# VectorE's remainder moved to the front of its step and GpSimd's half put behind it, in the second and third cross-attention; the three products of a chunk in another order

## The reference, cut to what matters

```python
x = x + L0_xattn(layernorm(x), ctx);  x = x + L0_ffn(layernorm(x))
x = x + L1_xattn(layernorm(x), ctx);  x = x + L1_ffn(layernorm(x))
x = x + L2_xattn(layernorm(x), ctx);  x = x + L2_ffn(layernorm(x))
x = x + L3_xattn(layernorm(x), ctx);  x = x + L3_ffn(layernorm(x))
# a cross-attention, for each batch element b and head h
scores = einsum('qd,kd->qk', q_h, k_h) * scale
out_h  = softmax(scores) @ v_h          # 56 queries, 1500 keys
```

## Time and profile before

| what | value |
|---|---|
| median of 3 runs | 3975.17 us (3973.31 to 3981.1) |
| the profiled execution, its own time | 3978.74 us |
| its span in the profile | 3976.6 us |
| granted TensorE clock, mean | 0.959 |
| `ci` 0, 1, 2, 3 in the span (first to last remainder) | about 70 to 835, 1224 to 1933, 2015 to 2702, 3110 to 3846 us |

### The profile page before, as it was taken

How to read it: one execution, slowest core, us unless ns; L and a number is a source line. 1 busy time by engine, 2 the same in 40 slices (tenths; PEclk the granted TensorE clock), 3 DMA queues, 4 the chain that set the end, 5 groups by cost and what they waited for, 6 DMA issues and landing times.

```text
span 3976.6 us, 126748 instructions
## 1 busy us (share of the span) xinstructions
PE 3630.8 (91%) x51275; PEld 2766.4 (70%) x51275; DVE 3270.3 (82%) x6773; ACT 2709.4 (68%) x5391; POOL 2100.8 (53%) x2087
## 2 busy tenths in 40 slices
PE   6999999989978999999789999996997999999987
PEld 4777777766645777777567777775775677777775
DVE  6988898868878999999789999997565788888863
ACT  4777777756646888888478888883452677777752
POOL 3666666669864655555555555563003344444551
PEclk9999999989988999999799999997997899999998
DMA  5333333224436555554155555540000221122100
GB/s 144 110 104 106 107 106 112 67 76 149 152 102 160 145 131 155 141 149 126 40 159 139 149 146 141 135 130 21 1 1 22 68 62 55 55 62 61 55 22 16
DMA packets 224592, 385.85 MB, mean 97 GB/s; under 512 B 71848, under 2 KB 127800, under 8 KB 222648
## 3 DMA queue, kind: packets, MB, share of 16 engines
q1 hardware_dynamic: 223560, 377.69, 34.6%
q10 hardware_dynamic: 448, 0.06, 0.0%
HBM read 252.30 MB, written 103.08 MB: 89 GB/s over the span
## 4 chain that ended last, share of the span: by engine, by line
PE 65%; DVE 24%; issue 5%; DMA 2%; ACT 2%; POOL 2%; SPq 1%; DVEq 0%; POOLq 0%; ACTq 0%
PE ps L208 62%; DVE wst L1185 7%; DVE wst L1158 3%; DVE wst L1155 3%; DVE cTs L997 2%; DVE relu L1155 2%; DVE diff L1163 1%; DVE xn L188 1%; POOL wst L592 1%; PE ps L2004 1%; PE ps L710 1%; PE ps L275 1%; DMA big<-headq 1%; PE ps L1533 0%; PE ps L264 0%
## 5 line engine op out<-in xcount | busy, mean ns | idle before, releaser
L592 POOL TENSOR_TENSOR wst<-wst 125x448 bf16<-125x448 f32 (+2 forms) x1536 | 1410.1, 918 | 1252.9 <-ACT wst L790 642.3
L208 PEld LDWEIGHTS ps<-cx,wst 125*128 125x128 bf16 x32256 | 1193.4, 98 | 242.2 <-DVE wst L1185 36.6
L208 PE MATMUL ps<-cx,wst 125*128 125x65 bf16 (+1 forms) x32256 | 1246.2, 193 | 18.0 <-DVE wst L1185 12.3
L790 ACT ACTIVATE wst<-ps 125x448 f32<-125x448 f32 x1536 | 752.6, 544 | 276.3 <-PE ps L208 274.5
L1129 ACT ACTIVATE wst<-ps 125x448 f32<-125x448 f32 x1536 | 751.1, 545 | 89.5 <-PE ps L208 80.5
L208 PE MATMUL ps<-big,cx 128*125 128x448 bf16 (+1 forms) x3072 | 714.4, 354 | 0.8 <-DMA big<-topT 0.8
L846 DVE TENSOR_TENSOR wst<-wst 125x640 bf16<-125x640 f32 (+1 forms) x768 | 646.8, 842 | 22.0 <-ACT wst L790 21.8
L1185 DVE TENSOR_TENSOR wst<-wst 125x448 bf16<-125x448 f32 x768 | 592.1, 773 | 4.3 <-ACT wst L1129 4.3
L208 PE MATMUL ps<-big 97*128 97x224 bf16 (+2 forms) x3872 | 582.7, 279 | 5.4 <-POOL big L1428 2.1
L208 PEld LDWEIGHTS ps<-big,cx 128*125 128x125 bf16 (+1 forms) x3072 | 417.3, 137 | 142.8 <-DMA big<-topT 1.6
L208 PEld LDWEIGHTS ps<-big 97*128 97x128 bf16 (+2 forms) x3872 | 374.9, 98 | 186.5 <-issue 4.4
(11 more groups left out here) (268 smaller groups left out, 5235.1 us busy)
## 6 DMA issues: line engine op xcount, KB each, us to landing
big<-headk SPq DMA_DIRECT2D x192, 375.0 KB, 5.4
headk<-cTs SPq DMA_DIRECT2D x128, 375.0 KB, 3.7
cx<-ctxT SPq DMA_DIRECT2D x96, 375.0 KB, 10.0
cx<-ctxN SPq DMA_DIRECT2D x64, 377.9 KB
cx<-in_ctxN SPq DMA_DIRECT2D x64, 375.0 KB
big<-big SPq DMA_DIRECT2D x384, 56.0 KB, 2.6
big<-headq SPq DMA_DIRECT2D x64, 224.0 KB, 7.0
ctxN<-cx SPq DMA_DIRECT2D x32, 377.9 KB
```

The source lines that it names most:

```text
L208: return t.matmul(o, l, r, start=start, stop=stop, skip_group_check=True)
L592: g.tensor_tensor(pl[r][0:KP, at:], pf[r][0:KP, at:], pf[r][0:KP, at:].bitcast(BF16)[:, 1::2], ALU.subtract).then_inc(s["plp"], 1)
L790: e.activation(pf[T % 3][0:KP, cols], bank(2 + n2 % 3, 448)[0:KP], ACT.Exp, scale=scale).then_inc(s["ev"], 1)
```

## The change

In `ci` 1 and 2 VectorE's remainder of tile `T-1` becomes the first thing of its step, ahead of `keys`, `top` and the first reduction. In `ci` 1 and 2 GpSimd's half of tile `T-1` also waits for the semaphore `pl`, that is, until VectorE's half of the same tile is done. In all four cross-attentions the first two products of a chunk change places: the one with 64 columns comes first (and clears the bank in the first chunk), the one with 65 second.

```diff
@@ pool_cross
                     w.wait_ge(s["ev"], evacuated(ci, T - 1) + 2)
+                    if ci in (1, 2):
+                        w.wait_ge(s["pl"], NT * ci + T)
                     g.tensor_tensor(pl[r][0:KP, at:], pf[r][0:KP, at:], pf[r][0:KP, at:].bitcast(BF16)[:, 1::2],
                                     ALU.subtract).then_inc(s["plp"], 1)
@@ pe_values
-                mm(t, o[:, at:at + 65], ph[:, cols], of[:, i, 0:65], i == 0 and j == 0, False)
-                mm(t, o[:, at:at + 64], ph[:, cols], of[:, i, 65:129], False, False)
+                mm(t, o[:, at:at + 64], ph[:, cols], of[:, i, 65:129], i == 0 and j == 0, False)
+                mm(t, o[:, at:at + 65], ph[:, cols], of[:, i, 0:65], False, False)
                 n = mm(t, o[:, at:at + 65], pl[r][0:KP, cols], of[:, i, 0:65], False, i == KT - 1)
@@ dve_head
             for T in range(-26, HEAD_LAST):
+                if 0 <= T - 1 < NT:
+                    r = (T - 1) % 3
+                    w.wait_ge(s["ev"], evacuated(ci, T - 1) + 1)
+                    to = SPLIT[ci]
+                    v.tensor_tensor(pl[r][0:KP, 0:to], pf[r][0:KP, 0:to], pf[r][0:KP, 0:to].bitcast(BF16)[:, 1::2],
+                                    ALU.subtract).then_inc(s["pl"], 1)
                 if (k := due(T, -18)) >= 0:
                     keys(k)
...
                     if items[0][0:1] in ("s", "r"):
                         reduce(k, items[0])
-                if 0 <= T - 1 < NT:
-                    r = (T - 1) % 3
-                    w.wait_ge(s["ev"], evacuated(ci, T - 1) + 1)
-                    to = SPLIT[ci]
-                    v.tensor_tensor(pl[r][0:KP, 0:to], pf[r][0:KP, 0:to], pf[r][0:KP, 0:to].bitcast(BF16)[:, 1::2],
-                                    ALU.subtract).then_inc(s["pl"], 1)
```

## The result

The changed kernel takes 3919.20 us as the median of four runs (3915.11 to 3922.52) against 3978.14 for the kernel before on the same chip. The ratio is 0.9847, 95% interval 0.9835 to 0.9858: 59 us faster, where 105 were forecast as the likeliest. Nearly all of it happens in `ci` 1 and 2.

The account below looks back on a forecast made before the run. TensorE, busy 91% and stalled by waits for VectorE in `ci` 1 and 2, was taken as the bound. 31 periods x 3.4 us = 105 us off 3976.6 gave 3870 as a median, own range 3835 to 3910, outer bounds 3825 to 3945.

Parts of the forecast that it names:

- A: The forecast itself: 3870 us, own range 3835 to 3910, bounds 2.3 to 4.5 us gained a period; chance 0.60.
- D: Order of the three products matters: weighted sum at 29.3 ns instead of 30.4, 35 us less, 3835; chance 0.06.
- Part 1: GpSimd's added wait in `ci` 1 and 2: remainder falls from 755 to about 620 ns, VectorE's load by 3.3 us a period.
- Part 2: VectorE's remainder first in its step: TensorE's waits fall from 5.4 to 1.1 us a period, gain taken as 3.4.
- 1412.40: TensorE's 0.69 us stall for VectorE's remainder, which stood behind the key difference and a reduction; forecast to go.
- the 1.27 us remainder: VectorE's remainder ahead of reduction L1155, for which TensorE stalled 0.65 us at 1414.27; that stall was forecast to go.
- 1406.66: TensorE's 1.03 us stall for reduction L1155, which had a 1.03 us remainder ahead of it; forecast to go.
- 1405.12: TensorE's 0.60 us stall for reduction L1158; forecast to stay.
- The key difference: VectorE's L1163, directly behind the remainder: taken at 405 ns with VectorE first, not 868; 0.9 us a period at stake.
- Part 3: New order of the three products per chunk: taken as 0, with 35 us possible either way.
- B: Stalls move: bank waits for reductions stay, only lengthened remainders give their excess back, 50 us gained, 3925; chance 0.17.
- C: GpSimd's half comes late for `pe_values`' fourth chunk, 0.75 us a step; at eight of 24 steps 4056; chance 0.06.

## Why the prediction was right in direction and half in size

The time lies between the outer bounds, 3825 and 3945, but above the 3835 to 3910 of the forecast proper (A), and the period is 42.26 us where 41.0 were forecast. A slip in the bounds: A's 3835 with D's 35 us taken off is 3800, not 3825.

**Part 1, the wait: the step that failed.** It is "The remainder falls from 755 to about 620 ns: 24 x 135 = 3.2 us of VectorE in a period". It rose to 820. The prediction asked only whether GpSimd's half meets VectorE's half of the same tile. Such meetings made 56 of the 125 us that the remainders lost before; and a half put behind VectorE's by 0.2 us and lasting 0.93 reaches past the reduction of 0.67 into the next remainder, which cost 161 us after. VectorE's load in the period fell by nothing (40.93 to 41.17) instead of by 3.3 us. With GpSimd's half cut short the time fell to 3878 and 3875 us, within 9 us of the forecast of 3870, and TensorE's waits for the reductions to 0.7 us a period, where 1.1 had been forecast. That experiment also spares GpSimd 0.3 us a step; no weight load waits for GpSimd in the period of the changed kernel, so in the body of a stage that is not where its gain comes from.

**Part 2, the place: the mechanism held, by stalls.** TensorE's waits for the remainder went (1.1 us to none). The wait at the start of `pe_values` at 1412.40 and the one behind the 1.27 us remainder have no counterpart of their size in the period after; that of 1406.66 is gone too. The stall of 1405.12 stayed, as said, at 0.99 instead of 0.6 us, and all waits for reductions came to 2.4 us instead of 1.1, since the remainder ahead of them is long. The prediction gave the place no price of its own. The runs give it two: 16 us alone, with the halves meeting, and, together with the wait, 47 us where most meetings are cut.

**The key difference: the duration right, its price too low.** Taken at 0.405 with VectorE first, measured 0.406. It was weighed against 0.868 and as load of VectorE, 0.9 us a period; without the wait it would have been 1.15, and TensorE waits for the difference itself (39.9 us over both stages in the run without the wait), for which the prediction had no term. Of all the wait's merits this is the largest, about 30 us.

**Part 3: right.** Taken as 0, measured 0 to 7 us. The 35 us of rival D are excluded either way.

**Rivals.** The result of 3919 is nearest to B in time (3925), but not by its mechanism: B expected the lengthened remainders to give their excess back and the bank waits to stay, and it is the excess that stayed while the bank waits fell from 4.3 to 2.4 us. C did not come to pass in the period, and the run with the wait alone shows that it was one queue position away. At the ends of the two stages it did: 10.9 us of waits for GpSimd's half against 4.8 before, which is up to 6 us of what the forecast lacks.

**Open.** The last 15 us of the wait's worth, outside the steps of the key difference, are shown only as sums of waits for L1160 (46.0 against 23.0 us in 560), not step by step. The meetings were taken away only by leaving work out, so what a whole kernel without them would take is an inference.

## What to carry to other kernels

When two engines hold each other up on some instructions, an added wait may not remove the meeting but move it, as here: add the delayed instruction's length to its new start and look which instruction of the other engine comes there next, in this tile or the one after. Here a wait behind the other engine's half paid only once that half was made early: test two such edits apart, since one alone was 71 us slower, the other 16 faster, and both 57 faster. What stands directly behind a contended instruction in the queue can pay more than the instruction itself, and so can the engine that reads its result. Before two traces are compared, look where each profiled execution lies among its runs: here 10 of 12 us may be nothing else.

## What the runs showed of the hardware

In the pairs read here the two engines hand over in the order of issue, one instruction at a time. With a remainder running, a GpSimd instruction issued during it went next, and the following VectorE instruction, ready at once, stood until GpSimd was done: a 0.41 us difference took 1.15 us. The Trainium skill, "SBUF — State Buffer", section "Who interferes with whom", says that issue order decides who blocks; by that rule the trace agrees, and the rows add that VectorE does not keep its turn for the next instruction in its queue. Where VectorE came second it ended 0.3 us (the difference) or 0.5 us (a remainder) behind GpSimd, less than the 0.41 and 0.61 us that each takes alone, as if a part of it ran before the wait. The reductions, whose input lies in PSUM, show no such meeting: the 448 of L1160 took 662 to 679 ns, 428 of them with GpSimd's half running beside them.
